# A DLRM tower on one core: one-hots handed over by half, layer 1 in two banks by turns, interactions stored by chunk

## The reference

```python
e = jnp.stack([tbl_0[ids[:, 0]], ..., tbl_25[ids[:, 25]]], axis=1)      # (2048, 26, 128)
combined = jnp.concatenate([dense[:, None, :], e], axis=1)              # (2048, 27, 128)
interactions = jnp.einsum('bfd,bgd->bfg', combined, combined)
iu, ju = jnp.triu_indices(27, k=1)                                      # 351 pairs
z = jnp.concatenate([dense, interactions[:, iu, ju]], axis=1)
h = jnp.concatenate([z, dense], axis=1)                                 # (2048, 607)
h = jnp.maximum(h @ W_top1 + b_top1, 0.0)                               # 607 -> 512
h = jnp.maximum(h @ W_top2 + b_top2, 0.0)                               # 512 -> 256
y = h @ W_top3                                                          # 256 -> 1
```

## Time and profile before

| | |
|---|---|
| median of three runs | 369.8 us |
| the profiled execution's own time | 367.45 us |
| its span (first to last instruction) | 365.5 us |
| TensorE busy, matmuls | 327.2 us, 90% |
| GpSimd busy | 248.3 us, 68% |
| VectorE busy | 240.4 us, 66% |
| ScalarE busy | 180.1 us, 49% |
| bytes moved | 45.66 MB, mean 125 GB/s |

### The profile page before, as it was taken

How to read it: one execution, slowest core, us unless ns; L and a number is a source line. 1 busy time by engine, 2 the same in 40 slices (tenths; PEclk the granted TensorE clock), 3 DMA queues, 4 the chain that set the end, 5 groups by cost and what they waited for, 6 DMA issues and landing times.

```text
span 365.5 us, 10327 instructions
## 1 busy us (share of the span) xinstructions
PE 327.2 (90%) x4192; PEld 311.3 (85%) x4192; DVE 240.4 (66%) x721; ACT 180.1 (49%) x359; POOL 248.3 (68%) x264
## 2 busy tenths in 40 slices
PE   0576778999999999999999999999999999999957
PEld 0565668989999999999999989999999999998845
DVE  3999975994469762994379662994289564962011
ACT  2354465446534563546534554546544464446324
POOL 2777777777777777777777777777777777771200
PEclk9999999999999999999999999999999999999989
DMA  7999478652366425652466425662367335520230
GB/s 185 245 242 232 136 204 197 147 156 75 95 129 182 96 69 118 165 136 74 101 136 173 92 71 122 148 151 66 102 133 182 88 85 121 132 71 18 36 84 0
DMA packets 51108, 45.66 MB, mean 125 GB/s; under 512 B 29814, under 2 KB 45174, under 8 KB 51062
## 3 DMA queue, kind: packets, MB, share of 16 engines
q1 hardware_dynamic: 41314, 26.76, 31.6%
q0 software_dynamic: 8320, 16.95, 18.8%
q10 hardware_dynamic: 1428, 1.30, 1.3%
HBM read 39.33 MB, written 5.65 MB: 123 GB/s over the span
## 4 chain that ended last, share of the span: by engine, by line
PE 43%; DVE 32%; POOL 8%; ACT 6%; issue 6%; DMA 4%; SPq 0%; ACTq 0%; DVEq 0%; POOLq 0%
DVE onehot L703 32%; PE ps_m L362 16%; PE ps_g L351 12%; PE ps_o L326 8%; POOL rows L307 8%; PE ps_t L336 3%; PE ps_m L387 2%; ACT emb L534 2%; ACT h L567 2%; DMA idx<-gather_ids 1%; DMA interaction_scratch<-inter 1%; ACT h_hi L569 1%; DMA rows<-tables,idx 1%; ACT inter L549 1%; PE ps_o L401 1%
## 5 line engine op out<-in xcount | busy, mean ns | idle before, releaser
L307 POOL DMA_INDIRECT rows<-tables,idx x256 | 245.6, 960 | 84.5 <-issue 77.2
L703 DVE TENSOR_SCALAR onehot<-oh_ids,rownum 125x256 fp32r<-125x256 int32 x640 | 200.1, 388 | 57.0 <-PE ps_o L326 52.0
L326 PE MATMUL ps_o<-onehot,tbl_hi 125*128 125x256 f32 x640 | 163.0, 294 | 25.2 <-DVE tbl_lo L689 22.4
L326 PE MATMUL ps_o<-onehot,tbl_lo 125*128 125x256 f32 x640 | 157.4, 285 | 0.0
L326 PEld LDWEIGHTS ps_o<-onehot,tbl_hi 125*128 125x128 f32 x640 | 123.7, 193 | 33.0 <-DVE tbl_lo L689 24.2
L326 PEld LDWEIGHTS ps_o<-onehot,tbl_lo 125*128 125x128 f32 x640 | 124.2, 194 | 0.0
L518 ACT ACTIVATE emb<-ps_o 128x256 f32<-128x256 f32 x80 | 49.1, 735 | 98.8 <-PE ps_o L326 96.1
L351 PE MATMUL ps_g<-emb 128*54 128x54 f32 x2048 | 56.6, 214 | 5.6 <-ACT inter L549 3.4
L351 PEld LDWEIGHTS ps_g<-emb 128*54 128x54 f32 x2048 | 53.7, 130 | 9.1 <-ACT inter L549 4.3
L534 ACT ACTIVATE emb<-ps_t 128x512 f32<-128x512 f32 x64 | 46.3, 727 | 7.4 <-PE ps_t L336 7.1
L549 ACT ACTIVATE inter<-ps_g 128x432 f32<-128x432 f32 x64 | 33.3, 536 | 17.1 <-PE ps_g L351 14.8
(11 more groups left out here) (54 smaller groups left out, 209.3 us busy)
## 6 DMA issues: line engine op xcount, KB each, us to landing
oh_ids<-onehot_ids SPq DMA_DIRECT2D x80, 128.0 KB
rows<-tables,idx POOLq DMA_INDIRECT x256
x<-interaction_scratch SPq DMA_DIRECT2D x24, 117.0 KB
interaction_scratch<-inter SPq DMA_DIRECT2D x30, 91.0 KB
inter<-small_tables SPq DMA_DIRECT2D x4, 448.0 KB
interaction_scratch<-inter SPq DMA_DIRECT2D x30, 42.2 KB
interaction_scratch<-inter SPq DMA_DIRECT2D x28, 39.0 KB
dense<-dense_e SPq DMA_DIRECT2D x8, 128.0 KB
```

The costliest lines, as they stand in the source:

```text
L307: pool.indirect_dma_start(rows[e][:, k, :], None, tables[k], bass.IndirectOffsetOnAxis(ap=idx[:, NG * hh + k:NG * hh + k + 1], axis=0),).t ...
L326: mm = pe.matmul(o, tbl[p][:, k, c, :], onehot[n % SLOTS_OH][:, c, :], start=(c + p == 0), stop=(c == TCHUNKS - 1 and p == 1))
L703: op = nc.vector.tensor_scalar(onehot[n % SLOTS_OH][:, c, :], oh_ids[0:TPART, n % IDS, :], rownum[:, c:c + 1], None, ALU.is_equal)
```

## The change

Five edits.

One-hots by half. `make_onehot` tells TensorE after four pieces and again after eight; `lookup` waits before pieces 0 and 4, and gives each half of the buffer back when it has used it. The counters of both semaphores run twice as fast, and the other users of them count by two.

Layer 1 in two banks by turns. Output n goes to bank n % 2, and ScalarE takes each output when it is done. Outputs 2 and 3 wait for the relu of the output two before, which shares their bank.

Interactions by chunk. Three bands of nine features and the wrapped part are stored, each with its own semaphore; chunk 0 waits for band 0 only, chunk c for band c and the wrapped part. A band holds the shifts that its chunk needs: 21, 17 and 8 columns by 9 rows in place of 26 by 14 and 12 by 13. In the last block SyncE and ScalarE store bands 0 and 1, and GpSimd the wrapped part and band 2.

First loads. The gather indices are issued first, the row numbers third.

Low parts. In block 0 the low part of table 9 is made ahead of one-hot 10. In the last layers 1 and 2 the products with the high part of `x` or `h` are done first, ahead of the wait for the low part.

```diff
@@ constants
+    PART = TCHUNKS // 2
-    BANDS = [(f, min(f + SHIFTS + 1, FEATURES)) for f in (0, SHIFTS + 1)]
-    STORES = (QUAD, 2 * QUAD)
+    BANDS = [(f, f + PAIR_F) for f in range(0, FEATURES, PAIR_F)]
+    WRAPPED = len(BANDS)
@@ def store_band(eng, i, b, quads, stored)
             f0, f1 = BANDS[b]
+            g1 = min(f1 + SHIFTS, FEATURES)
...
-                eng.dma_start(scratch[f0:f1, f0 + 1:FEATURES, q, :],
-                              inter[p + f0:p + f1, col + f0 + 1:col + FEATURES, :]).then_inc(stored, 16)
+                eng.dma_start(scratch[f0:f1, f0 + 1:g1, q, :],
+                              inter[p + f0:p + f1, col + f0 + 1:col + g1, :]).then_inc(stored[b], 16)
@@ def load_x(eng, i, c)
-            for b, (f0, f1) in enumerate(BANDS):
-                if PAIR_F * c < f1 and f0 < PAIR_F * (c + 1):
-                    last_band = 1 if (i, b) == (LAST, 1) else 0
-                    eng.wait_ge(inter_stored[b], 16 * (STORES[b] * (i + 1) - QUAD * last_band))
-                    if last_band:
-                        eng.wait_ge(last_band_stored, 16 * QUAD)
+            for b in (c, WRAPPED) if c > 0 else (c,):
+                if i == LAST and b >= 2:
+                    eng.wait_ge(last_stored[b], 16 * QUAD)
+                else:
+                    eng.wait_ge(inter_stored[b], 16 * QUAD * (i + 1))
@@ sync
+            load_idx(0, 0, 2 * NG)
+            load_ids(0)
             sp.dma_start(rownum[:, :], row_numbers).then_inc(rownum_loaded, 16)
-            load_ids(0)
-            load_idx(0, 0, 2 * NG)
...
-            store_band(sp, LAST, 0, range(0, 2), inter_stored[0])
-            store_wrapped(sp, LAST, range(0, 2), inter_stored[1])
+            for b in range(2):
+                store_band(sp, LAST, b, range(0, 2), inter_stored)
@@ gpsimd, after the last gather
-            store_band(pool, LAST, 1, range(QUAD), last_band_stored)
+            store_wrapped(pool, LAST, range(QUAD), last_stored)
+            store_band(pool, LAST, 2, range(QUAD), last_stored)
@@ tensor, def lookup(i, k)
-                pe.wait_ge(onehot_ready, n + 1)
...
                 for c in range(TCHUNKS):
+                    if c % PART == 0:
+                        pe.wait_ge(onehot_ready, 2 * n + c // PART + 1)
...
-                mm.then_inc(onehot_used, 1)
+                    if c % PART == PART - 1:
+                        mm.then_inc(onehot_used, 1)
@@ tensor, def layer1(m, n)
-                if n == 2:
+                if n == 1:
                     wait(pe, y_copied, m)
-                o = ps_m[n // 2][:, BLOCK * (n % 2):BLOCK * (n % 2 + 1)]
+                if n >= 2:
+                    pe.wait_ge(h1_ready, 2 * (K1 * m + n - 1))
+                o = ps_m[n % 2][:, BLOCK * (n // 2):BLOCK * (n // 2 + 1)]
@@ tensor, def last_layer1(chunks)
+                    pe.wait_ge(x_hi, XCHUNKS * LAST + k + 1)
+                    for n in range(K1):
+                        for a in range(2):
+                            pe.matmul(last_l1[n], w1r[a][0:r, c, 128 * n:128 * (n + 1)], xr[0][0:r, c, :],
+                                      start=(k + a == 0), stop=False)
                     pe.wait_ge(x_split, XCHUNKS * LAST + k + 1)
                     for n in range(K1):
-                        for a, b in ((0, 0), (0, 1), (1, 0)):
...
+                        mm = pe.matmul(last_l1[n], w1r[0][0:r, c, 128 * n:128 * (n + 1)], xr[1][0:r, c, :],
+                                       start=False, stop=(k == XCHUNKS - 1))
@@ scalar
-            def relus1(m, bank):
-                act.wait_ge(l1_done, K1 * m + 2 * bank + 2)
-                for n in (2 * bank, 2 * bank + 1):
-                    relu1(m, n, ps_m[bank][:, BLOCK * (n % 2):BLOCK * (n % 2 + 1)])
+            def relus1(m, pair):
+                for n in pair:
+                    act.wait_ge(l1_done, K1 * m + n + 1)
+                    relu1(m, n, ps_m[n % 2][:, BLOCK * (n // 2):BLOCK * (n // 2 + 1)])
@@ vector, def make_onehot(n)
-                wait(dve, onehot_used, n - SLOTS_OH + 1)
                 for c in range(TCHUNKS):
+                    if c % PART == 0:
+                        wait(dve, onehot_used, 2 * (n - SLOTS_OH) + c // PART + 1)
...
-                op.then_inc(onehot_ready, 1)
+                    if c % PART == PART - 1:
+                        op.then_inc(onehot_ready, 1)
@@ vector, block 0
             for k in range(NO):
-                make_onehot(k + 1)
+                if k + 1 < NO:
+                    make_onehot(k + 1)
                 split_lo(k)
+            make_onehot(NO)
             split_lo(NO)
```

More of the change, by code:

```diff
@@ L219, in load_ids @@
             def load_ids(n):
-                wait(sp, onehot_ready, n - IDS + 1)
+                wait(sp, onehot_ready, 2 * (n - IDS + 1))
                 i, k = divmod(n, NO)
@@ L239, in turn_interactions @@
                 load_x_dense(i)
[L240 to L242 removed]
+                for b in range(len(BANDS)):
+                    store_band(sp, i, b, range(QUAD), inter_stored)
+                store_wrapped(sp, i, range(QUAD), inter_stored)
                 load_ids(NO * (i + 1) + NO - 1)
@@ L396, in last_layer1 @@
                         pe.wait_ge(onehot_placed, 2 * NU * BLOCKS)
+                    r = PAIR_ROWS if c < PAIR_CHUNKS else 128
+                    pe.wait_ge(x_hi, XCHUNKS * LAST + k + 1)
[3 more added lines that the diff above has]
+                                      start=(k + a == 0), stop=False)
                     pe.wait_ge(x_split, XCHUNKS * LAST + k + 1)
-                    r = PAIR_ROWS if c < PAIR_CHUNKS else 128
                     for n in range(K1):
-                        for a, b in ((0, 0), (0, 1), (1, 0)):
-                            mm = pe.matmul(last_l1[n], w1r[a][0:r, c, 128 * n:128 * (n + 1)],
-                                           xr[b][0:r, c, :], start=(k + a + b == 0),
-                                           stop=(k == XCHUNKS - 1 and a == 1))
+                        mm = pe.matmul(last_l1[n], w1r[0][0:r, c, 128 * n:128 * (n + 1)], xr[1][0:r, c, :],
+                                       start=False, stop=(k == XCHUNKS - 1))
                         if k == XCHUNKS - 1:
@@ L409, in last_layer2 @@
                 for c in range(K1):
+                    pe.wait_ge(h1_ready, 2 * (K1 * LAST + c + 1))
+                    for n in range(K2):
+                        for a in range(2):
+                            pe.matmul(last_l2[n], w2r[a][:, c, 128 * n:128 * (n + 1)], h1r[0][:, c, :],
+                                      start=(c + a == 0), stop=False)
                     pe.wait_ge(h1_split, K1 * LAST + c + 1)
                     for n in range(K2):
-                        for a, b in ((0, 0), (0, 1), (1, 0)):
-                            mm = pe.matmul(last_l2[n], w2r[a][:, c, 128 * n:128 * (n + 1)],
-                                           h1r[b][:, c, :], start=(c + a + b == 0),
-                                           stop=(c == K1 - 1 and a == 1))
+                        mm = pe.matmul(last_l2[n], w2r[0][:, c, 128 * n:128 * (n + 1)], h1r[1][:, c, :],
+                                       start=False, stop=(c == K1 - 1))
                         if c == K1 - 1:
@@ L539, in copy_grams @@
                 if e == 0:
-                    wait(act, inter_stored[0], 16 * STORES[0] * i)
-                    wait(act, inter_stored[1], 16 * STORES[1] * i)
+                    for stored in inter_stored:
+                        wait(act, stored, 16 * QUAD * i)
                     if i == 0:
@@ L657, in last_body @@
                 copy_grams(b)
-                store_band(act, LAST, 0, range(2, QUAD), inter_stored[0])
-                store_wrapped(act, LAST, range(2, QUAD), inter_stored[1])
+                for b in range(2):
+                    store_band(act, LAST, b, range(2, QUAD), inter_stored)
                 relus2(m)
```

21 lines of the change are left out of this document (11 added, 10 removed).

## The result

The changed kernel takes 359.57 us (median of four runs, 357.80 to 359.68) where the kernel before took 369.89 in the same series: 0.9713 of it, interval 0.9673 to 0.9753. Run once more in a later series it took 358.69 against 369.01, again 0.9713 (0.9691 to 0.9734). The profiled execution took 359.68 (span 357.9, TensorE busy 91%). The forecast of 358.8 lies among the runs of both series. Its parts came out less well than its sum.

A forecast was written before the change was run, and what follows sets the result against it. TensorE was taken to bound the kernel, with GpSimd's gathers just behind. Gathers then limit the gain to 10.1 us; with 0.9 in the tail, 11.0 off the median 369.8 gives 358.8 us, range 355.8 to 363.8.

The forecast's parts named there:

- The lookups: Ten lookups at each block's head: one-hots handed over by half take them to 21.04 us, 7.2 us gained over seven blocks.
- Two banks: First Gram products after layer 1: alternating banks remove all seven stops at ScalarE's copy, 3.4 us gained.
- Block 0: Last lookup of block 0: table 9's low part comes 2.48 us earlier; 1.0 us counted, bounds 0 and 2.0.
- The index load: Kernel start: gather indices issued first let GpSimd start at 3.4 us, 3.8 earlier; at worst 0.84, at best 4.7.
- The first rival: Kernel start: the index load is not faster, only 0.84 us won, time 361.8 us; chance 0.15.
- The bound that decides: Last Gram products: gathers allow 6.3 + 3.8 = 10.1 us, TensorE 11.6; the smaller counts, TensorE waiting for gathers.
- the third rival: Last Gram products: TensorE's clock falls while it waits for the last gather, costing 1.7 us, time 360.5; chance 0.08.
- The stores and the last block: From the last copy to the end: shorter band 0 store and high-part order gain about 0.9 us, bounds -0.5 and 2.0.
- The narrow bands in the blocks before: Stores in earlier blocks: estimated to grow from 8.1 to 9.4 us, still hidden by 5.1 us of slack.
- The sum: Whole kernel: 10.1 + 0.9 = 11.0 us off, taken from the runs' median of 369.8, giving 358.8 us.

The follow-up runs named there:

- the tail filled in the kernel before: Kernel before with 7 and 20 matmuls of no use around layer 3 of block 6, while TensorE waits for the last block's first chunk: 367.72 us, 0.9962.

## Why the prediction was right, and where it was not

*The lookups: right.* 21.10 us against 21.04, no release of VectorE's one-hots left. Alone they bring the block from 40.7 to 39.95, and without them the change is worth 4.5 us (0.9877).

*Two banks: right, and a little small.* The stops at the copy are gone; the block goes from 40.7 to 40.27 alone (4.2 us in all seven blocks, 3.4 forecast). Both together give 39.42, and 0.77 + 0.45 is 1.22 of the 1.30: the two add up, since both are TensorE's own time.

*Block 0: wrong, and without effect.* 1.0 us was forecast. The last table's low part came earlier (done at 44.28, where TensorE's lookup started behind it at 46.73 in the earlier trace rows), but ScalarE, which places the transposed rows, then stood 3.93 us at a weight load before its conversion at 47.26:

```profile
47.26 1.06 ACT L517 ACTIVATE w_hi<-x 117x1024 fp32r<-117x1024 f32 x1 [3.93 <-DMA x<-w_pairs]
48.23 0.65 ACT L549 ACTIVATE emb<-ps_t 128x512 f32<-128x512 f32 x1
```

The Gram products began at 50.91 (51.28 in the earlier trace rows), at the lower clock (0.60 over the 4 us from 50), and block 1 at 59.66, 0.36 later than before. Block 1 has a bound of its own, which the forecast doesn't name: ahead of it TensorE waits for three small loads, layer 3's weights and two biases (`w3_biases_loaded`; `b2s` is the last). First the trace above, then that of the repeated run, where the clock stayed up in block 0:

```profile
59.66 0.39 PE L330 MATMUL ps_o<-onehot,tbl_hi 125*128 125x256 f32 x1 [0.43 <-DMA b2s<-b]
```

```profile
60.50 0.39 PE L330 MATMUL ps_o<-onehot,tbl_hi 125*128 125x256 f32 x1 [1.52 <-DMA b2s<-b]
```

Twelve of the fourteen traces have this wait, of 0.3 to 1.95 us, and block 1 starts at 59.30 to 61.33. The step that failed is "weight conversions on ScalarE whose loads only partly move": these loads held the Gram products, and the last small ones held block 1. It cost nothing, because the gathers catch up with TensorE later anyway. The low part's new place was not run alone.

*The index load: right in kind, too large.* The first rival (0.84 won) fell. The load lands 3.1 us after its issue and not 5.33 (KB, us from issue to landing):

```profile
idx<-gather_ids SPq DMA_DIRECT2D x1, 16.0 KB, 3.1
```

GpSimd started at 4.03 to 4.67 in all traces with this order. 3.8 were forecast from the row numbers' packets; 3.03 came at the first gather. At the last gather 3.1 and 2.7 were left in the two traces.

*The bound that decides: right.* From the last gather's issue to the last Gram products it was 10.02 us before (329.68 to 339.70) and is 3.94 now, 6.1 less, where 6.3 was forecast. With the 3.1 of the gathers that is 9.2 in place of 10.1. TensorE's own gain came out smaller too: without the 0.84 us that it waited for the last rows, its last Gram products would have started at 329.65, 10.0 earlier than before and not 11.6, mostly because block 0 gave -0.4 in place of 1.0. The two bounds end within a microsecond of each other.

*The clock: the third rival happened, in one execution.* With a chance of 0.08 it stood for 1.7 us; the last Gram products took 5.02 and not 3.48, 1.5 more. In all other traces they took 3.45 to 3.48. It is no rule of these stops.

*The stores and the last block: wrong.* 0.9 was forecast, in the pair of traces it is nothing (21.8 from the last copy to the end both times). The step that failed is the store by itself. It did shorten from 4.81 to 3.80, and that 1.0 was about the 0.9 taken. But the first chunk's load, counted at its old length, went from 2.69 to 3.86. GpSimd was still issuing its eight stores beside it:

```profile
336.55 2.51 POOL L197 DMA_DIRECT2D interaction_scratch<-inter  x4 [9.06 <-ACT inter L564]
339.04 2.25 POOL L188 DMA_DIRECT2D interaction_scratch<-inter  x4
```

That these stores are what slows the load is the reading of the two variants (old stores: long store, short load), not shown by itself.

*The narrow bands in the blocks before: hidden, as said.* SyncE's stores of block 2 take 8.51 us to the first chunk load (8.07 in the earlier trace rows):

```profile
98.80 6.35 SPq L188 DMA_DIRECT2D interaction_scratch<-inter  x12
105.19 1.65 SPq L197 DMA_DIRECT2D interaction_scratch<-inter  x4
...
107.31 3.05 SPq L217 DMA_DIRECT2D x<-interaction_scratch  x3
```

By the rule that the Trainium skill states (DMA: Bandwidth & Descriptors, section "Why a DMA increments its semaphore by 16 and not by 1"), the estimate was 9.4 for nine engines; by pieces alone it would have been 6.8. The measured 8.5 is between, and settles neither.

*The sum.* The two traces give 7.6 and 8.6 us of span (357.9 and 356.9 against 365.5), the medians 10.3, the forecast 11.0. In the first trace the sizes were too large by 0.9 in the gathers and 0.9 in the tail, and the clock took 1.5. The medians show more than the traces because the profiled execution of the kernel before was a quick one: at 367.45 it lies below all its 49 later runs (367.94 to 371.11). Most of those carry a second fall of the clock, worth 1.1 us, but that is not all of it: the eleven with its own mean clock, 0.995, still average 368.61. That execution is also one of the two traces without the wait ahead of block 1; the other, of the two banks alone, is the quickest of its six runs as well (363.83). Where TensorE bounds, a later block 1 comes out at the end: with it at 59.86 (the tail filled in the kernel before) and 60.47 (the index load first) in place of 59.30, the last Gram products start at 340.37 and 341.29 in place of 339.70. In the changed kernel's two traces block 1 is 0.84 apart and the last Gram products 0.44, as much as the last gather (0.43). So taking the 11.0 from the median and not from the profiled execution was lucky: a part of the distance between them seems to be time that only the kernel before loses. How large a part isn't shown.

## What to carry to other kernels

When the busiest engine is only just ahead of a second one, work out the second bound and its start before counting what the first can give. The same edit (the index load) was worth nothing before and 3 us after. A transfer that gets shorter is counted together with the next one: here the load grew by what the store had saved. A wait is only filled for nothing when the filling is surely shorter than the wait; where TensorE idled for microseconds ahead of a load, matmuls of no use kept the clock up and gave the kernel before 1.4 us.

## What was not expected of the hardware

The granted clock fell (0.58 over the 4 us from 330) in the last Gram products of one execution, after two stops of 0.84 and 0.75 us. In the repeated run of the same program, after 0.40 and 0.76, and in the variant with the old order of loads, after 0.88 and 0.76 at the same two places, it stayed at 1.00. And 256 gathers, nearly each issued 0.30 us after the one before, took 321.5 to 324.4 us from first to last in fourteen traces; in a kernel that waits for them, this spread goes into its time. Three loads of 1 to 2 KB, issued between 53 and 57 us, held TensorE in twelve traces, the last of them landing 3.7 to 4.6 us after its issue where the chain shows it.
